# A normalised layer with a spectral filter, a code correction and an FFN: another order of DVE's and ACT's work in the first two chunks, and one pair of sums moved from POOL to DVE

## The chip, the cores and the metric

One core of a Trainium2 chip runs the kernel. The metric is the device time of one execution in microseconds.

## The reference

The input x is 2 x 4096 tokens of 256 numbers. With `xn = layernorm(x)` over the 256 numbers, the result is `x + attn(xn) + ffn(xn)`:

- `ffn`: `gelu(xn @ w1 + b1) @ w2 + b2`, 256 to 1024 to 256.
- `attn`: a number D (a "fractal dimension") is computed from the first 1024 numbers of `xn`: for five prefix lengths, the count of values over the prefix's mean, and a slope of logarithms. D gives a filter of 256 frequencies; `x1` is the inverse FFT of the filtered FFT of every row, a circulant matrix product. 24 latents `x1 @ W_el + b_el` are cut to bits at zero, corrected by a code with 12 checks, and `attn = x1 + corrected @ W_le + b_le`.

## The kernel before

**Tiling.** The 8192 tokens are worked in 16 chunks of 512 (CTOK). A chunk is held transposed: 128 partitions x 2 halves of the row (KB) x 512 tokens. The 1024 hidden units are 8 blocks (MB), numbered m. To get fp32 accuracy, both factors of a product are split in a high part (a cast to fp32r, by ACT) and a low part (the subtraction, by DVE), and PE multiplies hi*hi, lo*hi and hi*lo.

**PE's order.** `up(c, par, m)` (L857, matmuls on L882) makes block m of the hidden layer of chunk c in p_h, and `down(c, m)` (L887, L900 and L905) adds it to p_f, two blocks later. In between stand `latents` (L919, L926: the 24 latents into p_l), `filtered` (L930: the circulant product into p_s), `checks` (L941: the code's products) and `le_products` (L952, L956: the corrected bits by W_le, added to p_s). Each engine runs its own list in program order; semaphores join them. Chunk 0 runs in an opening of its own (L1046 to L1075) in which the filter is being made, chunk 1 in `first_branch_chunk`, which also does the latents, the filter and the corrections of chunk 0; then a loop `chunk` does two chunks a turn, and `last_chunk` ends.

**What ACT, DVE and POOL do.** ACT: Gelu (L433), the high part of the hidden block (L441, `hidden_hi`), high part of the chunk's columns xn (L411, `columns_hi`), of uv (L418, `turned_hi`), the weights' high parts (L481, L486). DVE: the low parts: `hidden_lo` (L611), `columns_lo` (L601), `turned_lo` (L606), `w1_part_lo` (L732); the statistics of the next chunk (L569) and `aggregate` (L574); `centre` (L591) and `scale` (L596), which normalise the columns; `add_ffn` (L635), which adds p_f to the output and frees p_f for the next chunk; `take_bits` (L616), which cuts p_l to bits and frees p_l; `take_checks` (L628), `correct` (L623), and the additions of p_s. POOL: `inverse_root` (L346 to L351: 1/sqrt(var + eps) by a power) and `turn` (L363: uv, the sum and the difference of the two halves of the columns). SP issues the DMAs in its own order; `spread_rows` (L268) writes mean and 1/std to DRAM and reads them back broadcast to all partitions (L286).

**The opening on DVE and ACT.** The two lists are written out by hand: DVE's L750 to L844, ACT's L489 to L542. DVE mixes chunk 0's low parts with the filter's scalar steps (L782 to L811), the weights' low parts, and the preparation of chunk 1. The latents' rows are `le_t` (W_le's sums and differences, L822), split in three bf16 parts: le3 first part on ACT (L516), the rest `le_r1` on DVE (L828), `le_mid` and its copy on ACT (L540, L542), the last part on DVE (L842). `c_hi` and `c_lo` (L532, L834) are the circulant matrix, `cw` (L536 on ACT, L837 on DVE) the latents' weights by it; the latter's `c_ready` lets PE start `latents(0)`. `columns_lo(1, 1)` lets PE start `up(1, ...)`: its wait is on `t_lo` (L861). `latents(1)` waits for `bits_done` of chunk 0 (L922), `down(1, 0)` for `ffn_added` of chunk 0 (L892), `le_products(0)` for `cor_done` (L954). `xc0` are the columns of chunk 0, copied by ACT (L510) into rows_sb[0].

Of the kernel before, what the change touches and what calls it, by code (L numbers as in the profile page):

```python
# [8 lines left out]
ALU = mybir.AluOpType  # L9
# [4 lines left out]
TOKENS, E, HID, LAT, SYN = 2 * 4096, 256, 1024, 24, 12  # L14
# [54 lines left out]
def build(nc, x, xt, small, latent, w1, w2, ident, consts, basis, codes, out):  # L69
    ctx = ExitStack()  # L70
    with ctx:
# [17 lines left out]
        xc0 = rows_sb[0]  # L89
# [237 lines left out]
        def _(pool):  # L327
# [23 lines left out]
                nc.gpsimd.tensor_tensor(row_nums[par][:, 1, tiles], var_eps[:, tiles], minus_half[:, tiles],  # L351
                                        ALU.pow).then_inc(rstd_done, 1)

            def turn(c, first=False):

                if first:
                    pool.wait_ge(xc0_made, 1)
                else:
                    pool.wait_ge(scaled, c)
                    pool.wait_ge(u_lo, c)  # L360
                columns = xc0 if first else xn
                for k, op in enumerate((ALU.add, ALU.subtract)):
                    nc.gpsimd.tensor_tensor(uv[:, k, :], columns[:, 0, :], columns[:, 1, :], op).then_inc(turned, 1)  # L363


            for g in range(2):
# [21 lines left out]
            then(nc.gpsimd.tensor_tensor(series[:], series[:], weighted[:], ALU.mult))  # L388
            nc.gpsimd.tensor_tensor(filt_w[:], series[:, 0:KB], series[:, KB:2 * KB], ALU.mult).then_inc(filt_made, 1)

            turn(0, first=True)
            inverse_root(2 + HEAD, 0)
            turn(1)
            with pool.Fori(0, (CHUNKS - 4) // 2) as i:
# [8 lines left out]
        def _(act):  # L403
# [4 lines left out]
            def columns_hi(c, par):  # L408

                act.wait_ge(scaled, c)  # L410
                nc.scalar.copy(xT_hi[par][:, :, :], xn[:, :, :]).then_inc(t_hi, 1)  # L411
# [99 lines left out]
            last.then_inc(xc0_made, 1)  # L511
            gelu(0, 4, first=True)
            hidden_hi(0, 4, first=True)
            act.wait_ge(le_turned, 1)
            act.wait_ge(le_set, 1)
            nc.scalar.mul(le3[0:LAT, :, :], le_t[:], 0.5).then_inc(le_first, 1)  # L516
            gelu(0, 5, first=True)
            hidden_hi(0, 5, first=True)
            act.wait_ge(code_in, 16)
# [10 lines left out]
            made = p_l[:, 0:E].rearrange("p (a e) -> p a e", a=2)  # L530
            nc.scalar.copy(c_f[:, :, :], made).then_inc(c_copied, 1)
            nc.scalar.copy(c_hi[:, :, :], made).then_inc(c_hi_ready, 1)  # L532
            act.wait_ge(cw_made, 1)
            act.wait_ge(cw_set, 1)
            latent_made = p_g[:, SEG:SEG + KB * LAT].rearrange("p (k l) -> p k l", k=KB)
            nc.scalar.copy(cw[:, :, 0:LAT], latent_made).then_inc(cw_hi_ready, 1)  # L536
            columns_hi(1, 1)
            turned_hi(0, first=True)
            act.wait_ge(le_rest, 1)
            nc.scalar.copy(le_mid[:], le_r1[:]).then_inc(le_second, 1)  # L540
# [11 lines left out]
        def _(dve):  # L552
# [61 lines left out]
            def take_bits(c, par):  # L614
                dve.wait_ge(rest_done, c + 1)
                nc.vector.scalar_tensor_tensor(out=word[SEG * par:SEG * par + LAT, :], in0=p_l[0:LAT, :],  # L616
                                               scalar=latent_sb[:, 0:1], in1=rest[:],
                                               op0=ALU.add, op1=ALU.is_gt).then_inc(bits_done, 1)
# [12 lines left out]
            def add_ffn(c):  # L631
                dve.wait_ge(down_done, MB * (c + 1))
                for k in range(KB):
                    xc = columns(c)[:, k, :]
                    nc.vector.scalar_tensor_tensor(out=xc, in0=p_f[:, k, :], scalar=bias[:, k:k + 1], in1=xc,  # L635
                                                   op0=ALU.add, op1=ALU.add).then_inc(ffn_added, 1)
# [39 lines left out]
            def first_branch_chunk(c, par):  # L676
                b = c - 1
                statistics(c + 1, 1 - par)
                add_ffn(b)
                dve.wait_ge(stats_made, c + HEAD + 2)  # L680
                hidden_lo(c, 0)
                aggregate(1 - par)
                take_bits(b, 1 - par)
                hidden_lo(c, 1)
                hidden_lo(c, 2)
                turned_lo(c)
                take_checks(b)
                take_bits(c, par)
                hidden_lo(c, 3)
                centre(c + 1, 1 - par)  # L690
                scale(c + 1, 1 - par)
                hidden_lo(c, 4)
                correct(b)
                take_checks(c)
                columns_lo(c + 1, 1 - par)
                hidden_lo(c, 5)
                add_sums(b)
                hidden_lo(c, 6)
                add_differences(b)
                hidden_lo(c, 7)  # L700
# [64 lines left out]
            for g in range(2):  # L765
# [22 lines left out]
            then(nc.vector.tensor_tensor(fr_b[:], values, fr_s[:, 1, :].unsqueeze(2).broadcast_to(table), ALU.is_gt))  # L788
            then(nc.vector.tensor_tensor(fr_a[:], fr_b[:], masks, ALU.mult))
            nc.vector.tensor_reduce(fr_s[:, 2, :], fr_a[:], AX.X, ALU.add).then_inc(part_counts, 1)  # L790
            statistics(1, 1)
            hidden_lo(0, 1)
            w1_part_lo(2)
            dve.wait_ge(stats_made, 3)
            aggregate(1)
            hidden_lo(0, 2)
# [27 lines left out]
                                    ALU.subtract).then_inc(le_turned, 1)  # L824
            hidden_lo(0, 5)
            hidden_lo(0, 6)
            dve.wait_ge(le_first, 1)
            nc.vector.scalar_tensor_tensor(out=le_r1[:], in0=le_t[:], scalar=0.5, in1=le3[0:LAT, :, :],  # L828
                                           op0=ALU.mult, op1=ALU.subtract).then_inc(le_rest, 1)
            centre(1, 1)  # L830
            scale(1, 1)
            hidden_lo(0, 7)
            dve.wait_ge(c_hi_ready, 1)
            nc.vector.tensor_tensor(c_lo[:, :, :], c_f[:, :, :], c_hi[:, :, :].bitcast(F32), ALU.subtract)  # L834
            dve.wait_ge(cw_hi_ready, 1)
            latent_made = p_g[:, SEG:SEG + KB * LAT].rearrange("p (k l) -> p k l", k=KB)
            nc.vector.tensor_tensor(cw[:, :, SEG:SEG + LAT], latent_made, cw[:, :, 0:LAT].bitcast(F32),  # L837
                                    ALU.subtract).then_inc(c_ready, 1)
            columns_lo(1, 1)
            turned_lo(0)  # L840
            dve.wait_ge(le_second, 1)
            nc.vector.tensor_tensor(le3[2 * SEG:2 * SEG + LAT, :, :], le_r1[:], le_mid[:],  # L842
# [342 lines left out]
```

## Time and profile before

| | us |
|---|---|
| median of 3 runs | 418.75 (418.73 to 419.31) |
| the profiled execution, its own time | 418.89 |
| its span in the trace | 417.1 |
| PE busy | 409.1 (98%) |
| DVE busy | 307.3 (74%) |
| ACT busy | 218.7 (52%) |
| POOL busy | 73.7 (18%) |
| share of PE in the chain that ended last | 93% |

The span is the stretch from the first to the last instruction of the trace; the profiled execution took 1.8 us more than its span. The clock that PE was granted was 0.999 of its full speed over the span. In a timeline a row is one or several instructions of one kind in a row, with start and duration; brackets say how long the engine stood idle before it and what released it. Durations of successive instructions overlap a little, so that the pace is read from start to start.

### The profile page before, as it was taken

What the parts mean: (1) busy time and instruction counts of PE and PEld (TensorE: products, weight loads), DVE (VectorE), ACT (ScalarE), POOL (GpSimd) and SP (SyncE); (2) the same over time, 40 slices, a digit from 0 to 9 for tenths busy, and PEclk for the clock granted to TensorE, in tenths of its full rate; (3) what the DMA queues carried; (4) which work ended last, traced back from release to release, by engine and by line L of the source; (5) the groups of instructions that cost most, each with busy time, mean ns of one, the idle gap of its engine ahead of it and who ended that gap; (6) DMA issues with size and microseconds to landing.
All of it is one profiled execution on the core that took longest, in us unless ns stands there. A gap on an engine that the chain in (4) does not pass through costs nothing.

```text
span 417.1 us, 5569 instructions
## 1 busy us (share of the span) xinstructions
PE 409.1 (98%) x1789; PEld 325.8 (78%) x1789; DVE 307.3 (74%) x503; ACT 218.7 (52%) x325; POOL 73.7 (18%) x102
## 2 busy tenths in 40 slices
PE   8998999999999999999999999999999999999996
PEld 4786787887888788787887878788787878878774
DVE  7888696968669686776867778686786868676654
ACT  3957446555365554536555464554536655464641
POOL 2161321212012121111212012121111212012000
PEclk9999999999999999999999999999999999999999
DMA  7562223133331123332122332223333111111011
GB/s 221 200 210 95 101 61 92 52 101 103 101 101 56 51 95 101 101 101 72 53 76 101 101 101 90 26 86 101 101 101 98 53 51 51 51 51 50 2 50 50
DMA packets 16495, 36.04 MB, mean 86 GB/s; under 512 B 5452, under 2 KB 8164, under 8 KB 16484
## 3 DMA queue, kind: packets, MB, share of 16 engines
q1 hardware_dynamic: 16340, 35.78, 27.2%
q10 hardware_dynamic: 144, 0.13, 0.1%
q8 instruction: 5, 0.08, 0.1%
q14 instruction: 6, 0.05, 0.1%
HBM read 27.45 MB, written 8.45 MB: 86 GB/s over the span
## 4 chain that ended last, share of the span: by engine, by line
PE 93%; DVE 4%; DMA 1%; issue 1%; ACT 0%; POOL 0%; SPq 0%; DVEq 0%
PE p_h L882 41%; PE p_f L900 27%; PE p_f L905 13%; PE p_s L937 5%; PE p_l L926 3%; PE p_s L956 2%; PE p_g L950 1%; DMA x_sb<-x 1%; DVE stats L569 1%; DVE xt_sb L644 0%; DVE xt_sb L650 0%; DVE xT_lo L601 0%; DVE w_lo L732 0%; DVE h_lo L611 0%; DVE xt_sb L726 0%
## 5 line engine op out<-in xcount | busy, mean ns | idle before, releaser
L433 ACT ACTIVATE h<-p_h,small_sb 128x512 f32<-128x512 f32 x128 | 88.1, 688 | 155.1 <-PE p_h L882 155.0
L611 DVE TENSOR_TENSOR h_lo<-h,h_hi 128x512 fp32r<-128x512 f32 x128 | 90.1, 704 | 71.4 <-ACT h_hi L441 71.2
L900 PE MATMUL p_f<-h_hi,w_hi 128*128 128x512 f32 x254 | 99.7, 392 | 0.0
L900 PE MATMUL p_f<-h_hi,w_lo 128*128 128x512 f32 x254 | 99.0, 390 | 0.0
L882 PE MATMUL p_h<-xT_hi,w_hi 128*128 128x512 f32 (+1 forms) x258 | 86.1, 415 | 1.5 <-DVE xT_lo L601 1.0
L441 ACT CAST h_hi<-h 128x512 fp32r<-128x512 f32 x128 | 79.4, 620 | 5.8
L882 PE MATMUL p_h<-xT_lo,w_hi 128*128 128x512 f32 (+1 forms) x258 | 79.6, 390 | 0.1
L882 PE MATMUL p_h<-xT_hi,w_lo 128*128 128x512 f32 (+1 forms) x258 | 79.5, 389 | 0.0
L905 PE MATMUL p_f<-h_lo,w_hi 128*128 128x512 f32 x254 | 78.2, 389 | 0.0
L363 POOL TENSOR_TENSOR uv<-xn 128x512 f32<-128x512 f32 x30 | 43.6, 1475 | 127.7 <-DVE xn L596 127.7
L882 PEld LDWEIGHTS p_h<-xT_hi,w_hi 128*128 128x128 f32 x258 | 48.3, 189 | 11.9 <-DVE xT_lo L601 1.5
L882 PEld LDWEIGHTS p_h<-xT_lo,w_hi 128*128 128x128 f32 x258 | 48.3, 188 | 10.8 <-DVE xT_lo L767 0.3
L882 PEld LDWEIGHTS p_h<-xT_hi,w_lo 128*128 128x128 f32 x258 | 48.3, 188 | 10.7
L900 PEld LDWEIGHTS p_f<-h_hi,w_hi 128*128 128x128 f32 x254 | 47.7, 188 | 10.3
L905 PEld LDWEIGHTS p_f<-h_lo,w_hi 128*128 128x128 f32 x254 | 47.7, 188 | 10.1
L900 PEld LDWEIGHTS p_f<-h_hi,w_lo 128*128 128x128 f32 x254 | 47.7, 188 | 10.0
L346 POOL TENSOR_TENSOR var_eps<-mv,eps 128x4 f32<-128x4 f32 (+1 forms) x17 | 3.9, 227 | 173.3 <-DVE mv L574 173.3
L601 DVE TENSOR_TENSOR xT_lo<-xn,xT_hi 128x1024 fp32r<-128x1024 f32 x15 | 32.7, 2179 | 0.8 <-ACT xT_hi L411 0.7
L635 DVE SCALAR_TENSOR_TENSOR xt_sb<-p_f,bias,xt_sb 128x512 f32 (+1 forms) x30 | 21.1, 746 | 12.5 <-PE p_f L905 12.5
L606 DVE TENSOR_TENSOR uv_lo<-uv,uv_hi 128x1024 fp32r<-128x1024 f32 x16 | 19.6, 1226 | 9.2 <-ACT uv_hi L418 9.2
L411 ACT CAST xT_hi<-xn 128x1024 fp32r<-128x1024 f32 x15 | 15.8, 1054 | 13.5 <-DVE xn L596 13.5
L591 DVE TENSOR_TENSOR xn<-xt_sb,rows_sb 128x1024 f32<-128x1024 f32 x15 | 18.3, 1223 | 5.9 <-DMA rows_sb<-rows_dram 5.5
(117 smaller groups left out, 331.4 us busy)
## 6 DMA issues: line engine op xcount, KB each, us to landing
xt_sb<-xt SPq DMA_DIRECT2D x16, 512.0 KB, 5.2
x_sb<-x SPq DMA_DIRECT2D x15, 512.0 KB, 4.5
rows_sb<-rows_dram SPq DMA_DIRECT2D x15, 512.0 KB, 4.1
out<-xt_sb SPq DMA_DIRECT2D x15, 512.0 KB, 2.9
xt_sb<-w SPq DMA_DIRECT2D x3, 512.0 KB, 7.3
xt_sb<-w SPq DMA_DIRECT2D x2, 256.0 KB, 4.1
basis_sb<-basis SPq DMA_DIRECT2D x1, 384.0 KB, 8.8
x_sb<-x SPq DMA_DIRECT2D x2, 128.0 KB, 2.1
```

The costliest lines, as they stand in the source:

```text
L363: nc.gpsimd.tensor_tensor(uv[:, k, :], columns[:, 0, :], columns[:, 1, :], op).then_inc(turned, 1)
L433: nc.scalar.activation(h[m % 2][:], p_h[:, m % 2, :], ACT.Gelu, bias=small_sb[:, S_B1 + m:S_B1 + m + 1]).then_inc(gelu_done, 1)
L441: nc.scalar.copy(h_hi[m % HR][:], h[m % 2][:]).then_inc(h_hi_done, 1)
L591: nc.vector.tensor_tensor(xn[:, :, :], columns(c), to_halves(rows_sb[par][:, 0, :]), ALU.subtract).then_inc(centred, 1)
L601: nc.vector.tensor_tensor(xT_lo[par][:, :, :], xn[:, :, :], xT_hi[par][:, :, :].bitcast(F32), ALU.subtract).then_inc(t_lo, 1)
L606: nc.vector.tensor_tensor(uv_lo[:, :, :], uv[:, :, :], uv_hi[:, :, :].bitcast(F32), ALU.subtract).then_inc(u_lo, 1)
L611: nc.vector.tensor_tensor(h_lo[m % HR][:], h[m % 2][:], h_hi[m % HR][:].bitcast(F32), ALU.subtract).then_inc(h_lo_done, 1)
L635: nc.vector.scalar_tensor_tensor(out=xc, in0=p_f[:, k, :], scalar=bias[:, k:k + 1], in1=xc, op0=ALU.add, op1=ALU.add).then_inc(ffn_added, 1)
L882: last = mm(p_h[:, m % 2, tok], w[:, k, m * P:(m + 1) * P], xp[par][:, k, tok], start=(n == 0), stop=(n == 3 * KB - 1))
L900: mm(p_f[:, a, :], w[:, m, a * HF:(a + 1) * HF], h_hi[r][:], start=(m == 0 and w is w2_hi), stop=False, skip_group_check=True)
L905: last = mm(p_f[:, a, :], w2_hi[:, m, a * HF:(a + 1) * HF], h_lo[r][:], start=False, stop=(m == MB - 1), skip_group_check=True)
L937: last = mm(p_s[:, k, :], w[:, k, :], xp[:, k, :], start=(n == 0), stop=False, skip_group_check=True)
```

## The change

On POOL, `turn(0)` is gone; DVE makes the two sums of chunk 0 itself. On ACT, the first part of the latents' rows (le3, `le_first`) is made after `columns_hi(1, 1)`, which itself stands ahead of the wait for `cw_made`. On DVE, in the opening: `w1_part_lo(2)` and `hidden_lo(0, 1)` stand ahead of `statistics(1, 1)`; `le_r1` is made after `cw`, `columns_lo(1, 1)` before it, with the two sums between. In `first_branch_chunk`, `add_ffn(0)` stands after `take_bits(0)`.

```diff
--- before.py
+++ after.py
@@ -351,16 +351,12 @@
                 nc.gpsimd.tensor_tensor(row_nums[par][:, 1, tiles], var_eps[:, tiles], minus_half[:, tiles],
                                         ALU.pow).then_inc(rstd_done, 1)
 
-            def turn(c, first=False):
-
-                if first:
-                    pool.wait_ge(xc0_made, 1)
-                else:
-                    pool.wait_ge(scaled, c)
-                    pool.wait_ge(u_lo, c)
-                columns = xc0 if first else xn
+            def turn(c):
+
+                pool.wait_ge(scaled, c)
+                pool.wait_ge(u_lo, c)
                 for k, op in enumerate((ALU.add, ALU.subtract)):
-                    nc.gpsimd.tensor_tensor(uv[:, k, :], columns[:, 0, :], columns[:, 1, :], op).then_inc(turned, 1)
+                    nc.gpsimd.tensor_tensor(uv[:, k, :], xn[:, 0, :], xn[:, 1, :], op).then_inc(turned, 1)
 
 
             for g in range(2):
@@ -388,7 +384,6 @@
             then(nc.gpsimd.tensor_tensor(series[:], series[:], weighted[:], ALU.mult))
             nc.gpsimd.tensor_tensor(filt_w[:], series[:, 0:KB], series[:, KB:2 * KB], ALU.mult).then_inc(filt_made, 1)
 
-            turn(0, first=True)
             inverse_root(2 + HEAD, 0)
             turn(1)
             with pool.Fori(0, (CHUNKS - 4) // 2) as i:
@@ -511,9 +506,6 @@
             last.then_inc(xc0_made, 1)
             gelu(0, 4, first=True)
             hidden_hi(0, 4, first=True)
-            act.wait_ge(le_turned, 1)
-            act.wait_ge(le_set, 1)
-            nc.scalar.mul(le3[0:LAT, :, :], le_t[:], 0.5).then_inc(le_first, 1)
             gelu(0, 5, first=True)
             hidden_hi(0, 5, first=True)
             act.wait_ge(code_in, 16)
@@ -530,11 +522,14 @@
             made = p_l[:, 0:E].rearrange("p (a e) -> p a e", a=2)
             nc.scalar.copy(c_f[:, :, :], made).then_inc(c_copied, 1)
             nc.scalar.copy(c_hi[:, :, :], made).then_inc(c_hi_ready, 1)
+            columns_hi(1, 1)
+            act.wait_ge(le_turned, 1)
+            act.wait_ge(le_set, 1)
+            nc.scalar.mul(le3[0:LAT, :, :], le_t[:], 0.5).then_inc(le_first, 1)
             act.wait_ge(cw_made, 1)
             act.wait_ge(cw_set, 1)
             latent_made = p_g[:, SEG:SEG + KB * LAT].rearrange("p (k l) -> p k l", k=KB)
             nc.scalar.copy(cw[:, :, 0:LAT], latent_made).then_inc(cw_hi_ready, 1)
-            columns_hi(1, 1)
             turned_hi(0, first=True)
             act.wait_ge(le_rest, 1)
             nc.scalar.copy(le_mid[:], le_r1[:]).then_inc(le_second, 1)
@@ -676,11 +671,11 @@
             def first_branch_chunk(c, par):
                 b = c - 1
                 statistics(c + 1, 1 - par)
-                add_ffn(b)
                 dve.wait_ge(stats_made, c + HEAD + 2)
                 hidden_lo(c, 0)
                 aggregate(1 - par)
                 take_bits(b, 1 - par)
+                add_ffn(b)
                 hidden_lo(c, 1)
                 hidden_lo(c, 2)
                 turned_lo(c)
@@ -788,9 +783,9 @@
             then(nc.vector.tensor_tensor(fr_b[:], values, fr_s[:, 1, :].unsqueeze(2).broadcast_to(table), ALU.is_gt))
             then(nc.vector.tensor_tensor(fr_a[:], fr_b[:], masks, ALU.mult))
             nc.vector.tensor_reduce(fr_s[:, 2, :], fr_a[:], AX.X, ALU.add).then_inc(part_counts, 1)
+            w1_part_lo(2)
+            hidden_lo(0, 1)
             statistics(1, 1)
-            hidden_lo(0, 1)
-            w1_part_lo(2)
             dve.wait_ge(stats_made, 3)
             aggregate(1)
             hidden_lo(0, 2)
@@ -824,19 +819,23 @@
                                     ALU.subtract).then_inc(le_turned, 1)
             hidden_lo(0, 5)
             hidden_lo(0, 6)
-            dve.wait_ge(le_first, 1)
-            nc.vector.scalar_tensor_tensor(out=le_r1[:], in0=le_t[:], scalar=0.5, in1=le3[0:LAT, :, :],
-                                           op0=ALU.mult, op1=ALU.subtract).then_inc(le_rest, 1)
             centre(1, 1)
             scale(1, 1)
             hidden_lo(0, 7)
             dve.wait_ge(c_hi_ready, 1)
             nc.vector.tensor_tensor(c_lo[:, :, :], c_f[:, :, :], c_hi[:, :, :].bitcast(F32), ALU.subtract)
+            columns_lo(1, 1)
+
+            dve.wait_ge(xc0_made, 1)
+            for k, op in enumerate((ALU.add, ALU.subtract)):
+                nc.vector.tensor_tensor(uv[:, k, :], xc0[:, 0, :], xc0[:, 1, :], op).then_inc(turned, 1)
             dve.wait_ge(cw_hi_ready, 1)
             latent_made = p_g[:, SEG:SEG + KB * LAT].rearrange("p (k l) -> p k l", k=KB)
             nc.vector.tensor_tensor(cw[:, :, SEG:SEG + LAT], latent_made, cw[:, :, 0:LAT].bitcast(F32),
                                     ALU.subtract).then_inc(c_ready, 1)
-            columns_lo(1, 1)
+            dve.wait_ge(le_first, 1)
+            nc.vector.scalar_tensor_tensor(out=le_r1[:], in0=le_t[:], scalar=0.5, in1=le3[0:LAT, :, :],
+                                           op0=ALU.mult, op1=ALU.subtract).then_inc(le_rest, 1)
             turned_lo(0)
             dve.wait_ge(le_second, 1)
             nc.vector.tensor_tensor(le3[2 * SEG:2 * SEG + LAT, :, :], le_r1[:], le_mid[:],
```

## Rows read from the trace of the kernel before

**Rows 1.** Table by stage for PE: stretch, PE busy, matmuls, granted clock, DMA share, GB/s.

```profile
16.00:42.00 26.00, 24.00 (x110) 1.00 0.38 124
42.00:392.00 350.00, 350.00 (x1533) 1.00 0.25 78
```

**Rows 2.** Timeline of PE around its three gaps: start, duration, line, tiles, idle before.

```profile
15.86 0.28 PE L1042 MATMUL p_g<-fr_s,ones 128*128 128x5 f32 x2
16.59 0.73 PE L882 MATMUL p_h<-xT_hi,w_hi 128*128 128x512 f32 x2 [0.46 <-DVE w_lo L732]
...
19.43 0.28 PE L1042 MATMUL p_g<-fr_d,ones 128*128 128x1 f32 x2
19.57 0.71 PE L882 MATMUL p_h<-xT_hi,w_hi 128*128 128x512 f32 x2
...
33.33 0.62 PE L905 MATMUL p_f<-h_lo,w_hi 128*128 128x512 f32 x2
34.98 0.73 PE L882 MATMUL p_h<-xT_hi,w_hi 128*128 128x512 f32 x2 [1.02 <-DVE xT_lo L601]
35.54 0.62 PE L882 MATMUL p_h<-xT_hi,w_lo 128*128 128x512 f32 x2
...
39.69 0.61 PE L882 MATMUL p_h<-xT_lo,w_hi 128*128 128x512 f32 x2
40.82 0.73 PE L926 MATMUL p_l<-xT_hi,cw 128*128 128x512 f32 x2 [0.52 <-DVE word L616]
41.40 0.62 PE L926 MATMUL p_l<-xT_lo,cw 128*128 128x512 f32 x2
41.86 0.40 PE L937 MATMUL p_s<-uv_hi,c_hi 128*128 128x512 f32 x1
```

**Rows 3.** Timeline of ACT, the same columns.

```profile
13.36 0.61 ACT L481 CAST w_hi<-xt_sb 128x512 fp32r<-128x512 f32 x1
...
23.18 0.42 ACT L516 ACTIVATE le<-le_t 24x256 bf16<-24x256 f32 x1 [2.53 <-DVE le_t L823]
...
29.20 0.38 ACT L532 CAST c_hi<-p_l 128x256 fp32r<-128x256 f32 x1
...
44.85 1.05 ACT L418 CAST uv_hi<-uv 128x1024 fp32r<-128x1024 f32 x1 [2.20 <-POOL uv L363]
```

**Rows 4.** DVE's L611 from 24 to 34 us: ns min/median/max, first and last start.

```profile
L611 DVE TENSOR_TENSOR h_lo<-h,h_hi x3: 687/1766/1776, 24.9 to 31.0; 128x512 fp32r<-128x512 f32 x3
```

**Rows 5.** POOL's L363, ns min/median/max and starts, and its timeline in chunk 1.

```profile
L363 POOL TENSOR_TENSOR uv<-rows_sb x2: 1291/1519/1747, 24.8 to 26.0; 128x512 f32<-128x512 f32 x2
...
42.23 2.58 POOL L363 TENSOR_TENSOR uv<-xn 128x512 f32<-128x512 f32 x2
```

**Rows 6.** Timeline of DVE from 28 to 53 us.

```profile
28.58 1.21 DVE L591 TENSOR_TENSOR xn<-xt_sb,rows_sb 128x1024 f32<-128x1024 f32 x1
...
33.70 1.23 DVE L601 TENSOR_TENSOR xT_lo<-xn,xT_hi 128x1024 fp32r<-128x1024 f32 x1 [0.74 <-ACT xT_hi L411]
...
36.54 1.40 DVE L569 BATCH_NORM_STATS2 stats<-x_sb 128x6 f32<-128x256 f32 x4
37.86 1.39 DVE L635 SCALAR_TENSOR_TENSOR xt_sb<-p_f,bias,xt_sb 128x512 f32<-128x512 f32 x2
...
40.06 0.71 DVE L616 SCALAR_TENSOR_TENSOR word<-p_l,latent_sb,rest 24x512 bf16<-24x512 f32 x1
...
45.93 1.23 DVE L606 TENSOR_TENSOR uv_lo<-uv,uv_hi 128x1024 fp32r<-128x1024 f32 x1 [3.52 <-ACT uv_hi L418]
...
52.29 0.68 DVE L623 TENSOR_SCALAR cor<-p_g 96x512 bf16<-96x512 uint32 x1
```

**Rows 7.** SP's broadcast of the rows' numbers (L286): issue ns, first start, us to landing.

```profile
L286 SPq DMA_DIRECT2D rows_sb<-rows_dram x15: 319/320/333, 21.1 to 368.7; - x15
...
DMA to landing us min/median/max: 3.6/4.1/4.9
```

**Rows 8.** PE's timeline where chunk 0's corrections are multiplied.

```profile
53.36 0.60 PE L956 MATMUL p_s<-cor,le 96*128 96x512 bf16 x2
```

## The prediction

> **What bounds the kernel now.** I read the table by stage first. From 42 to 392 us PE is busy in 350.00 of 350 us, at a granted clock of 1.00; from 16 to 42 us it is busy in 24.00 of 26 us [rows 1]. So the loop is a solid block of matmuls, and whatever PE gains before 42 us it keeps to the end, as long as nothing else falls behind. The 2.00 us missing from 16 to 42 us are three gaps, which PE's timeline shows in brackets: 0.46 us ahead of `up(0, 4)`, released by the low part of w1; 1.02 us ahead of `up(1, 0)`, released by `columns_lo(1)`; 0.52 us ahead of `latents(1)`, released by `take_bits(0)` [rows 2]. All three wait for DVE. The change touches exactly the DVE work ahead of each.
>
> **What a gap costs.** Idle time understates it, because a matmul behind a wait also hides nothing of its weights' load. I therefore go from start to start. First gap: after the two 5-column matmuls the next start comes 0.73 us later (15.86 to 16.59); the same pair with no wait behind it takes 0.14 us (19.43 to 19.57). Loss 0.59. Second: 33.33 to 34.98 is 1.65, and 34.98 to 35.54 is 0.56, where two pairs without a wait are 0.46 apart (41.40 to 41.86); 1.65 + 0.56 - 0.92 = 1.29. Third: 39.69 to 40.82 is 1.13, then 0.58 to 41.40; 1.71 - 0.92 = 0.79 [rows 2]. The sum is 2.67 us by starts and 2.00 by idle brackets; I take 2.67, since starts are what shifts the block behind, and keep 2.00 as the lower bound of what three closed gaps bring.
>
> **Part 1, w1's low part ahead of hidden_lo(0, 1) and statistics(1).** ACT has the high part at 13.36 + 0.61 = 13.97 [rows 3]. In the order before, four statistics (1.3 us start to start, as 36.54 to 37.86 [rows 6]) and one `hidden_lo` (0.6 to 0.69) stand ahead of it; without them the low part is ready some 1.9 us earlier, at about 14.7, where PE wants it at 16.59 - 0.59 = 16.0. The gap closes, gain 0.59. `hidden_lo(0, 1)` also comes earlier; the statistics end at about 16.5 where the low part ended before, so everything behind them on DVE stays where it was. PE then reaches its later steps 0.59 earlier; by the timeline of DVE I expect none of them to be late.
>
> **Part 2, POOL's sums of chunk 0 go.** POOL made them from 24.8 us on, in 1291 and 1747 ns [rows 5]. Beside them two `hidden_lo` took 1766 and 1776 ns where the third of the same shape took 687 [rows 4]. I read this as the two engines hindering each other: 2 x 1.08 = 2.16 us of DVE's time. With POOL silent this is saved, and it lies on the path to the second gap. The page SBUF — State Buffer of the Trainium skill (section Who interferes with whom) says that a DVE instruction with two SBUF inputs and a GpSimd instruction that reads SBUF exclude one another, whichever is first holding the other up; by that rule the rows are two instructions taking turns, and the trace agrees in its size (a delay of 1.08 beside a POOL operation of 1.29).
>
> **Part 3, ACT.** ACT stood idle for 2.53 us before le3's first part, for `le_t` [rows 3]. Moved back, this wait no longer holds up the Gelu of block 5, and with it blocks 6 and 7 and the scaling of the basis. PE does not wait for them either way, so in itself it is worth nothing; it lets DVE have `hidden_lo(0, 5)` and `(0, 6)` done between 25.4 and, if ACT gained nothing on block 6, 27.1. The 0.42 of le3 now sits behind `columns_hi(1)`, in ACT's wait for `cw_made`, where ACT has nothing else.
>
> **Part 4, chunk 1's columns.** `centre(1)` needs the broadcast rows: issued at 21.1, landing 3.6 to 4.9 later [rows 7], so at 26.0 at the latest. It began at 28.58 [rows 6] and can now begin at 25.4 to 27.1. With `scale` it takes 2.45 (each as the 1.21), so xn is there at 27.9 to 29.5. ACT is free for `columns_hi(1)` when c_hi is made, which PE sets: 29.20 + 0.38 - 0.59 = 28.99 [rows 3]. The cast takes 1.05, as uv's does [rows 3], so 30.0; `columns_lo` 1.23 [rows 6], done at 31.2, or at 31.8 at the latest by the bounds above. PE wants it at 33.79 - 0.59 = 33.2. The second gap closes with 1.4 to 2.0 us to spare; gain 1.29.
>
> **Part 5, the sums on DVE.** No row shows them there. The nearest is `hidden_lo`, the same 128x512 in fp32 with two SBUF inputs: 0.687, which I take (0.6 start to start); the upper bound is a pair held up by another engine, 1.776 [rows 4], the lower nothing. They stand from 31.1 to 32.4. Behind them wait: `cw`'s low part, on which `latents(0)` hangs (ready at 32.6 or so, wanted 1.4 after `up(1, 0)`, at 34.6: covered); ACT's `turned_hi(0)`, 32.4 to 33.5; `turned_lo(0)`, then le's last part, `statistics(2)`. From `columns_lo` to the statistics it was 36.54 - 33.70 = 2.84 [rows 6]; less one subtraction of 1.14 start to start, 1.7 remain, so the statistics start at 33.5 + 1.7 = 35.2 instead of 36.54. le_r1 (0.33) falls into DVE's wait for uv_hi. SP's broadcast for chunk 2 waits for `turned` too, but before that for chunk 2's 1/std, which is later.
>
> **Part 6, add_ffn behind take_bits.** Between the statistics and the bits stood 40.06 - 36.54 = 3.52 us, of which add_ffn about 1.31 (its two of 0.7) [rows 6]. Without it the bits start at 35.2 + 2.2 = 37.4 and are there at 38.1. PE, 1.88 us earlier than before, wants them at 40.15 - 1.88 = 38.27. That is the tightest point of the sum: the margin is 0.1 to 0.2, and the weights' load wants to start 0.2 before. I count 0.1 lost and 0.69 gained. add_ffn then runs until 39.5; `down(1, 0)` wants it after `latents(1)` and `filtered(0)` (0.93 + 1.4), at 40.6. Covered by 1.1.
>
> **What is late next.** POOL's `turn(1)` hangs on `aggregate`, which moves with the bits. From the bits' start to `turned_lo(1)` it was 45.93 - 40.06 = 5.87, with 2.20 of ACT's wait for POOL in it; from there DVE ran without a pause to `correct(0)`, done 7.04 later at 52.97 [rows 3, 6]. PE used it at 53.36 [rows 8], 0.39 later. Now: 37.4 + 5.87 + 7.04 = 50.3, wanted at 53.36 - 2.67 = 50.7. The margin stays 0.4, if POOL takes no longer. It took 2.58 beside an idle DVE [rows 5], and will now meet `hidden_lo(1, 1)` and `(1, 2)`; its first pair took 1291 + 1747 beside such work, so up to 0.4 more: just covered. By the rule of the page named above, two `hidden_lo` would each wait for a POOL operation, which delays them but no product of PE; add_ffn, with one large SBUF input, would not be held.
>
> **The sum.** 0.59 + 1.29 + 0.69 = 2.57. The profiled execution took 418.89, so 416.3; the median of the runs is 0.14 under it, so 416.2 in the median. A difference of 0.2% (0.84 us) is about what a measurement of this kernel can tell from none.
>
> **Rivals.**
> A, the forecast: 416.2, with 415.9 if the third gap vanishes whole and the pairs run a little closer, 416.75 if only the bracketed idle time (2.00) comes back. Chance 0.70.
> B, bits still late: `take_bits(0)` takes the third gap's place because the sums, ACT's cast and `turned_lo` in front of the statistics come out 0.5 to 1 us longer than my sum of nine steps. Against it, each has its row. Time 418.75 - 1.88 to 418.75 - 2.1: 416.7 to 417.1. Chance 0.14.
> C, a new wait at `le_products(0)` or `down(1, 0)`: the margin of 0.4 is spent because POOL and DVE hold each other up around 39 to 43 us. If add_ffn is held for two POOL operations (2 x 1.29 less the margin of 1.1), 1.5 us come back as a wait: 417.7. If only turn(1) is slower by 0.8, 0.4 comes back: 416.6. Chance 0.08.
> D, DVE's 1.77 was not POOL's doing but that of the DMA then running: then the two `hidden_lo` stay slow and the sums take 1.77 each, 2.3 more than counted. `centre` at 26.6 to 27.1, bits at 40.5, third gap 2.3 instead of 0.79: the total gain is 0.3 us, 418.4. Against it: `centre` at 28.58 took its ordinary 1.21 [rows 6] while loads were under way. Chance 0.05. That the change moves no gap at all is in this case.
> E, slower: the sums on DVE are each held up by an operation as long as POOL's longest, 0.69 + 1.75 = 2.44. Place: between `columns_lo(1)` and `turned_lo(0)`. Every step from there to the bits moves 2 x (2.44 - 0.6) = 3.7; less the margin of 0.1 the third gap becomes 3.6 and the gain is 2.67 - 3.7 = -1.0: 419.8. It decides from 1.9 to 2.0 us a sum upward. Against it: POOL has no instruction between the filter's last and chunk 2's inverse root, so there is no one to hold them up. Chance 0.03.
>
> **The numbers.** The likeliest case gives 416.2. The range takes in A and B, and the milder half of C: 415.8 to 417.3. Faster by over 0.2% (under 417.9) are A, B and most of C: 0.91. Within 0.2%: D and the worst of C, 0.06. Slower: E, 0.03.
>
> **What the profile after would show.** Right: PE without a bracket at `up(0, 4)` and `up(1, 0)`, and one of at most 0.2 at `latents(1)`; busy 26.00 of 26 us at 16 to 42, or nearly; the two `hidden_lo` of blocks 5 and 6 at 0.69; DVE's sums at 0.69 each by 32.5 us; bits at 37.4; no wait of PE at L956 and L900; PE's block from 62 us on unchanged and 2.6 us earlier. Wrong, if a gap of over 0.3 us stands at `latents(1)` (B), at L956 or at `down(1, 0)` (C), if `hidden_lo` stays at 1.77 (D), or if the loop has gaps that it hasn't now.

## The result, and the profile after

| | before | after |
|---|---|---|
| median of 22 runs each, us | 418.88 (418.68 to 419.42) | 417.61 (416.46 to 420.66) |
| profiled execution: its time, its span | 418.89, 417.1 | 417.44, 415.6 |
| PE busy | 409.1 | 407.7 |
| DVE, ACT, POOL busy | 307.3, 218.7, 73.7 | 309.0, 218.9, 73.0 |

The ratio is 0.9973, 95% interval 0.9966 to 0.998: the change is faster, by 1.27 us, where the forecast was 2.6. The measured median lies 0.3 us above the range. The runs of the changed kernel also scatter more.

Table by stage for PE of the changed kernel, the columns of [rows 1]:

```profile
16.00:42.00 26.00, 25.13 (x114) 1.00 0.38 125
42.00:392.00 350.00, 350.00 (x1533) 1.00 0.25 78
```

The loop is still solid. From 16 to 42 us 0.87 us are missing where 2.00 were, and all of it is one new gap. PE's timeline of the changed kernel, with the starts that answer to [rows 2] (every line number is one lower):

```profile
15.77 0.28 PE L1041 MATMUL p_g<-fr_s,ones 128*128 128x5 f32 x2
15.90 0.71 PE L881 MATMUL p_h<-xT_hi,w_hi 128*128 128x512 f32 x2
...
26.75 0.61 PE L904 MATMUL p_f<-h_lo,w_hi 128*128 128x512 f32 x2
28.23 1.13 PE L1024 MATMUL p_l<-basis_w,basis_sb 128*128 128x256 f32 x4 [0.87 <-ACT basis_w L518]
29.01 0.59 PE L899 MATMUL p_f<-h_hi,w_hi 128*128 128x512 f32 x1
...
33.80 0.62 PE L904 MATMUL p_f<-h_lo,w_hi 128*128 128x512 f32 x2
34.25 0.62 PE L881 MATMUL p_h<-xT_hi,w_hi 128*128 128x512 f32 x2
...
38.88 0.61 PE L881 MATMUL p_h<-xT_lo,w_hi 128*128 128x512 f32 x2
39.38 0.73 PE L925 MATMUL p_l<-xT_hi,cw 128*128 128x512 f32 x2
39.95 0.63 PE L925 MATMUL p_l<-xT_lo,cw 128*128 128x512 f32 x2
...
51.90 0.61 PE L955 MATMUL p_s<-cor,le 96*128 96x512 bf16 x2
```

The product of the basis by the filter's weights, which makes the circulant matrix (L1024, called the circulant product from here on), stood without a gap in the kernel before:

```profile
27.41 0.62 PE L905 MATMUL p_f<-h_lo,w_hi 128*128 128x512 f32 x2
27.87 1.03 PE L1025 MATMUL p_l<-basis_w,basis_sb 128*128 128x256 f32 x4
28.55 0.59 PE L900 MATMUL p_f<-h_hi,w_hi 128*128 128x512 f32 x1
```

Laid beside the starts of before, PE's lead grows and shrinks in steps. It is 0.09 us at 15.77, which is luck of the opening. The first gap is closed: +0.60. Ahead of the circulant product the lead is 0.66 us (26.75 against 27.41); behind it PE is 0.46 us late (29.01 against 28.55): -1.12. The second gap is closed: +1.29. The third is closed but for 0.15: +0.63. With 0.03 lost in between, that leaves 1.46 us at `le_products(0)` (53.36 against 51.90). So the three terms of the sum were 0.60, 1.29 and 0.63 where 0.59, 1.29 and 0.69 were forecast, and a fourth, -1.12, was missing.

Where it comes from stands in the timelines of POOL, ACT and DVE of the changed kernel:

```profile
22.88 1.08 POOL L376 TENSOR_TENSOR quads<-quads,con 128x16 f32<-128x16 f32 x1
...
24.75 0.69 POOL L382 TENSOR_TENSOR series<-halves,powers 128x4 f32<-128x4 f32 x1
...
26.08 1.10 POOL L385 TENSOR_TENSOR filt_w<-series 128x2 f32<-128x2 f32 x1
```

```profile
27.27 0.91 ACT L518 ACTIVATE basis_w<-basis_sb,filt_w 128x256 f32<-128x256 f32 x2 [2.61 <-POOL filt_w L385]
```

```profile
23.21 0.67 DVE L606 TENSOR_TENSOR h_lo<-h,h_hi 128x512 fp32r<-128x512 f32 x1
24.69 0.69 DVE L606 TENSOR_TENSOR h_lo<-h,h_hi 128x512 fp32r<-128x512 f32 x1 [0.81 <-ACT h_hi L436]
25.90 1.23 DVE L586 TENSOR_TENSOR xn<-xt_sb,rows_sb 128x1024 f32<-128x1024 f32 x1 [0.51 <-DMA rows_sb<-rows_dram]
```

POOL makes the filter in twelve small steps. Three of them, of 16, 4 and 2 columns, took 1.08, 0.69 and 1.10 us; each is open while a wide DVE subtraction with two inputs in SBUF runs, and ends just behind it (23.88 + 0.08, 25.38 + 0.06, 27.13 + 0.05). Their neighbours take 0.20. POOL's starts say the same as its durations: the step behind the first of the three starts 1.16 us after it (24.04), in e1 below 0.35 (23.18 to 23.53). In the kernel before the same three steps took 0.27, 0.20 and 0.19, and from 23.15 to 24.86 DVE stood idle behind ACT, which had waited for `le_t` [rows 3]; POOL, then DVE:

```profile
20.59 1.11 POOL L376 TENSOR_TENSOR powers<-angle 128x4 f32<-128x4 f32 x1 [2.01 <-DVE angle L811]
21.78 0.52 POOL L377 TENSOR_TENSOR powers<-powers 128x4 f32<-128x4 f32 x1
...
22.74 0.27 POOL L380 TENSOR_TENSOR quads<-quads,con 128x16 f32<-128x16 f32 x1
...
24.64 0.19 POOL L389 TENSOR_TENSOR filt_w<-series 128x2 f32<-128x2 f32 x1
```

```profile
20.43 1.22 DVE L738 TENSOR_TENSOR w_lo<-xt_sb,w_hi 128x1024 fp32r<-128x1024 f32 x1
21.56 0.69 DVE L611 TENSOR_TENSOR h_lo<-h,h_hi 128x512 fp32r<-128x512 f32 x1
...
24.86 3.47 DVE L611 TENSOR_TENSOR h_lo<-h,h_hi 128x512 fp32r<-128x512 f32 x2 [1.70 <-ACT h_hi L441]
```

DVE's subtraction began at 24.86, when the filter was made (24.83). Now ACT begins the Gelu of block 5 2.9 us earlier (20.58 against 23.51), DVE follows, the filter is late (27.18), ACT scales the basis late and PE waits.

These rows also show that the filter's path was held up already in the kernel before. Its first two steps, of 4 columns each, took 1.11 and 0.52 us and ended 0.05 us behind DVE's w_lo (21.65) and `hidden_lo` (22.25), both wide and with two SBUF inputs. They have these lengths, and end 0.05 to 0.06 us behind DVE's, in the traces of all fourteen kernels here, e1 too. Measured against the usual 0.20 that is 1.2 us, an estimate from these rows; no run took them apart from DVE's work.

### The profile page after: what moved, and what is told of

Read it like the earlier page. It is cut to its first block, busy times and chain, and to the rows that moved or that the text cites. A ratio compares the mean times of both kernels' runs of the same rounds, so it can differ in the third digit from the quotient of the medians.

```text
span 415.6 us, 5569 instructions
## 1 busy us (share of the span) xinstructions
PE 407.7 (98%) x1789; PEld 325.6 (78%) x1789; DVE 309.0 (74%) x505; ACT 218.9 (53%) x325; POOL 73.0 (18%) x100
## 3 DMA queue, kind: packets, MB, share of 16 engines
HBM read 27.45 MB, written 8.45 MB: 86 GB/s over the span
## 4 chain that ended last, share of the span: by engine, by line
PE 96%; DVE 1%; DMA 1%; POOL 0%; issue 0%; ACT 0%; DVEq 0%; SPq 0%; ACTq 0%; POOLq 0%
PE p_h L881 43%; PE p_f L899 28%; PE p_f L904 14%; PE p_s L936 5%; PE p_l L925 4%; PE p_s L955 2%; PE p_g L949 1%; DMA x_sb<-x 1%; POOL row_nums L351 0%; DVE xt_sb L639 0%; DVE xt_sb L645 0%; DVE xt_sb L721 0%; PE p_l L1024 0%; DVE rows_sb L740 0%; PE p_s L1054 0%
## 5 line engine op out<-in xcount | busy, mean ns | idle before, releaser
L359 POOL TENSOR_TENSOR uv<-xn 128x512 f32<-128x512 f32 x30 | 44.5, 1502 | 128.1 <-DVE xn L591 128.1
```

Of the source, the lines that this page charges most:

```text
L359: nc.gpsimd.tensor_tensor(uv[:, k, :], xn[:, 0, :], xn[:, 1, :], op).then_inc(turned, 1)
```

## The experiments

In the table, "opening taken out" is the time on PE from the first 5-column product (12.86 us in the trace before) to `le_products(0)` (53.36), which leaves out what differs before the first and includes all three old gaps. Each is from one trace. The ratios are against runs of the kernel before in the same rounds, whose medians were 418.78 to 418.97.

| kernel | median, us | ratio, 95% interval | opening taken out, us |
|---|---|---|---|
| before | 418.88 | | 40.50 |
| the change | 417.61 | 0.9973, 0.9966 to 0.998 | 39.13 |
| e1, filter first | 416.44 | 0.9940, 0.9926 to 0.9954 | 38.09 |
| e2, filter before centre | 417.04 | 0.9953, 0.9940 to 0.9967 | 38.23 |
| e3, latents' rows back | 417.40 | 0.9965, 0.9951 to 0.9978 | 38.99 |
| e7, e1 with POOL's sums | 416.47 | 0.9946, 0.9932 to 0.9959 | 38.12 |
| e4, columns only | 417.72 | 0.9976, 0.9966 to 0.9985 | 39.38 |
| e5, w1 only | 418.57 | 0.9995, 0.9986 to 1.0004 | 40.16 |
| e6, bits first only | 418.21 | 0.9986, 0.9977 to 0.9995 | 39.94 |
| e10, those three together | 417.38 | 0.9957, 0.9943 to 0.9970 | 38.60 |
| e11, sums only | 418.92 | 0.9997, 0.9988 to 1.0007 | 40.52 |
| e12, latents' rows only | 418.84 | 0.9996, 0.9984 to 1.0007 | 40.48 |
| e8, two SBUF inputs | 417.81, one run | | 39.52 |
| e9, one PSUM input | 416.71, one run | | 38.01 |

### Is it DVE's work that delays the filter?

**e1** adds one wait to the changed kernel:

```diff
+            dve.wait_ge(filt_made, 1)
             hidden_lo(0, 5)
             hidden_lo(0, 6)
```

Expected: 

> The changed kernel, with one wait more on DVE: hidden_lo(0, 5) of the first chunk waits until POOL has made the filter. Theory (POOL's filter steps are held up by DVE's two-input subtractions, 2.35 us in the changed kernel, and PE waits for the scaled basis for 1.13 us): filter at 25.0 instead of 27.2 us, all of POOL's small steps at 0.2 us, no wait of PE ahead of the circulant product, time 1.1 us under the changed kernel, about 416.4 to 416.6 us, and a narrower spread of the runs. Rival (the delay of the filter is POOL's own, or comes from DMA): filter still at 27, time 417.6 or more, since DVE is now idle as well.

POOL's same three steps in e1, and DVE behind them:

```profile
23.18 0.28 POOL L376 TENSOR_TENSOR quads<-quads,con 128x16 f32<-128x16 f32 x1
...
24.25 0.20 POOL L382 TENSOR_TENSOR series<-halves,powers 128x4 f32<-128x4 f32 x1
...
25.09 0.20 POOL L385 TENSOR_TENSOR filt_w<-series 128x2 f32<-128x2 f32 x1
```

```profile
25.32 1.29 DVE L606 TENSOR_TENSOR h_lo<-h,h_hi 128x512 fp32r<-128x512 f32 x2 [1.73 <-POOL filt_w L385]
```

```profile
16.00:42.00 26.00, 26.00 (x120) 1.00 0.38 126
```

DVE now stands idle for 1.73 us ahead of these two, and the kernel is 1.2 us faster than the change: 416.44, 0.2 above what was forecast for the change. PE is busy in 26.00 of 26 us, and no time goes at the circulant product (1.14 us from the pair ahead of it to the matmul behind it, as before). The five runs lie within 0.4 us. Not all of POOL's small steps are short, as was expected: the first two keep 1.11 and 0.52.

**e2** puts the same wait two lines lower, behind `hidden_lo(0, 6)`.

Expected: 

> The changed kernel, with DVE waiting for the filter only after hidden_lo(0, 6), before centre(1). Theory: the last POOL step keeps its 0.2 us instead of 1.10, the two earlier ones stay long (1.08 and 0.69), filter at about 26.3, PE waits 0.1 to 0.3 ahead of the circulant product: about 416.7 us, between e1 and the changed kernel. Rival as in e1: no gain, 417.6.

```profile
22.95 1.08 POOL L376 TENSOR_TENSOR quads<-quads,con 128x16 f32<-128x16 f32 x1
...
24.82 0.72 POOL L382 TENSOR_TENSOR series<-halves,powers 128x4 f32<-128x4 f32 x1
...
26.18 0.20 POOL L385 TENSOR_TENSOR filt_w<-series 128x2 f32<-128x2 f32 x1
```

Two steps stay long, the third, which had met `centre(1)`, is short, and PE loses 0.23 us at the circulant product, too little for a bracket. The median, 417.04, is between e1 and the change, so that half of the loss is gone by the medians. By the one trace, which is of a run of 416.61, 0.90 of 1.04 us is gone (38.23 against 39.13 and 38.09). What the slower runs of e2 lose isn't shown.

**e8 and e9** ask which DVE work does it. Both are e1 with two additions into an unused tile in DVE's idle time; they differ in one operand (each kernel has one of the two lines marked e8 and e9):

```diff
+            dve.wait_ge(xc0_made, 1)
+            for k in range(KB):
+                nc.vector.tensor_tensor(scrap[:, k, :], xc0[:, 1 - k, :], xc0[:, k, :], ALU.add)   # e8
+                nc.vector.tensor_tensor(scrap[:, k, :], p_s[:, k, :], xc0[:, k, :], ALU.add)       # e9
             dve.wait_ge(filt_made, 1)
```

Expected of e8: 

> e1 with two more DVE additions of 128x512 ahead of its wait for the filter, at about 23.2 to 24.5 us, both inputs in SBUF, results unused. Theory of exclusion: one or two of POOL's small steps grow by 0.5 to 0.7 us each, the filter comes at 25.6 to 26.4, one of the additions may take longer. Rival: no effect on POOL.

Expected of e9: 

> As e8, but one input of each addition is in PSUM. Theory of exclusion by the second SBUF input: POOL's steps keep 0.2 us, the filter at 25.0 as in e1. Rival (any DVE work hinders POOL): as in e8.

The additions and the POOL step beside them, e8 and then e9:

```profile
23.06 1.68 POOL L377 TENSOR_TENSOR quads<-quads,con 128x16 f32<-128x16 f32 x1
...
23.39 1.27 DVE L823 TENSOR_TENSOR scrap<-rows_sb 128x512 f32<-128x512 f32 x2
```

```profile
23.29 0.27 POOL L377 TENSOR_TENSOR quads<-quads,con 128x16 f32<-128x16 f32 x1
...
23.63 1.27 DVE L823 TENSOR_TENSOR scrap<-p_s,rows_sb 128x512 f32<-128x512 f32 x2
```

With both inputs in SBUF a POOL step of 0.27 us waits through both additions, 1.68 us, and the filter comes at 26.58, a little later than expected. With one input in PSUM the POOL steps that follow at the same time (23.64 to 25.39) all keep 0.20, the filter comes at 25.39, and the additions take the same 1.27. It is not DVE being busy; it is the second SBUF input. DVE's additions lose nothing here. SBUF — State Buffer of the Trainium skill states in Who interferes with whom that a DVE instruction with two SBUF inputs contends with a GpSimd instruction that reads SBUF, and that one with at most one SBUF input, outside the two-port modes (which `tensor_tensor` hasn't), does not; e8 and e9 agree with both halves. Downstream e8 loses 0.54 us at the circulant product, and the bits are late (a wait of 0.87 at `latents(1)`), which is the same delay handed on through DVE's own wait.

### Which parts of the change were worth something?

**e3** is the changed kernel with the three lines of le3's first part back ahead of `gelu(0, 5)`.

Expected: 

> The changed kernel, with the latents' first rows on ACT back ahead of Gelu block 5 of the first chunk (one part of the change undone). Theory: ACT then hands DVE blocks 5 and 6 at 24.9 and 26.4, after POOL's filter steps, which keep 0.2 us each; the basis is in time; DVE's own chain ends later, so that the gap at latents(1) is 0.4 to 0.6: about 416.7 to 416.9 us. Rival (ACT's earlier Gelu is what closes the gap at up(1, 0)): a gap comes back there, 417.6 or more.

POOL's steps are short again (filter at 24.97), since `hidden_lo(0, 5)` starts at 25.00. In return DVE's chain ends later:

```profile
39.10 0.73 PE L925 MATMUL p_l<-xT_hi,cw 128*128 128x512 f32 x2 [0.45 <-DVE word L611]
```

By its bracket the gap is of the size expected; from start to start it costs 0.72 us, where e7 loses 0.04 there and the change 0.15. Another 0.22 goes at the circulant product, for which ACT, with the latents' rows in front, has the basis ready only as PE wants it (27.32 against 27.26), and 0.19 before it, mostly at `up(0, 7)` (24.36 and 24.95). The median, 417.40, is therefore above the 416.7 to 416.9 expected. By its trace e3 is 0.14 us better than the change (38.99 against 39.13), by its median 0.2, which the intervals don't separate. So the move of the latents' rows costs PE 0.7 us up to the circulant product (1.12 against 0.22 + 0.19) and gives back 0.6 at `latents(1)` (0.15 against 0.72): on balance about nothing, but as the difference of a cost that the forecast left out and a gain on DVE's chain.

**e7** is e1 with the change's other large part undone, POOL makes chunk 0's sums behind the filter.

Expected: 

> e1, but POOL makes chunk 0's two sums again, after the filter, as in the kernel before. Theory A (the sums on POOL cost DVE 2.2 us on the path to the columns of chunk 1): hidden_lo of blocks 5 and 6 take 1.77 each again, columns_lo ends near 33 where PE wants it at 33.2, but DVE saves the 1.2 us of sums behind it: 0 to 0.5 us slower than e1, 416.4 to 417.0. Theory B (the move of the sums is what brought the gain): 417.7 or more.

```profile
25.05 3.45 DVE L611 TENSOR_TENSOR h_lo<-h,h_hi 128x512 fp32r<-128x512 f32 x2 [1.71 <-POOL filt_w L389]
28.42 1.21 DVE L591 TENSOR_TENSOR xn<-xt_sb,rows_sb 128x1024 f32<-128x1024 f32 x1
...
32.01 1.23 DVE L601 TENSOR_TENSOR xT_lo<-xn,xT_hi 128x1024 fp32r<-128x1024 f32 x1 [0.17 <-ACT xT_hi L411]
```

The subtractions are slow again and the columns are ready at 33.24, just when PE wants them (33.2), which costs 0.25 us from start to start at `up(1, 0)`; the 1.2 us that DVE saves behind them make up for it: the bits start as long after the opening as in e1 (37.63 - 12.78 against 37.86 - 13.06), and 0.04 us is lost at `latents(1)` where e1 loses 0.22. The median is e1's within the noise. So the move of the sums is worth nothing that these runs can tell once the filter is protected.

**e11** is the kernel before with the sums alone moved to DVE, behind `c_lo`; **e4** the kernel before with chunk 1's columns alone moved:

```diff
             nc.scalar.copy(c_hi[:, :, :], made).then_inc(c_hi_ready, 1)
+            columns_hi(1, 1)
             act.wait_ge(cw_made, 1)
...
-            columns_hi(1, 1)
...
             nc.vector.tensor_tensor(c_lo[:, :, :], c_f[:, :, :], c_hi[:, :, :].bitcast(F32), ALU.subtract)
+            columns_lo(1, 1)
...
-            columns_lo(1, 1)
```

Expected of e11: 

> The kernel before, with only the two sums of chunk 0 moved from POOL to DVE, behind c_lo. Theory: hidden_lo of blocks 5 and 6 fall from 1.77 to 0.69 us and centre starts 1.5 to 2 us earlier, but ACT's columns_hi(1) still stands behind the wait for the latents' weights (32.6): the gap at up(1, 0) stays at 1.0, time as before, 418.7 to 418.9. Rival (the prediction's step: the 2.16 us saved lie on the path to that gap): the gap closes, 417.5.

Expected of e4: 

> The kernel before, with only chunk 1's columns moved: on ACT columns_hi(1) ahead of the wait for the latents' weights, on DVE columns_lo(1) behind c_lo. POOL keeps the sums. Theory (in the kernel before ACT's order held the columns back, not POOL's sums on DVE): columns_hi at 31.1 instead of 32.6, the gap ahead of up(1, 0) closes (1.29), the gap at latents(1) stays at 0.7 to 0.8: 417.5 us. Rival, as the prediction put it (the 2.2 us of slow subtractions lie on that path): little gain, 418.5 or more.

e11, timelines of DVE, ACT and PE:

```profile
26.39 0.69 DVE L606 TENSOR_TENSOR h_lo<-h,h_hi 128x512 fp32r<-128x512 f32 x1 [0.85 <-ACT h_hi L436]
27.00 0.41 DVE L823 SCALAR_TENSOR_TENSOR le_r<-le_t,le 24x256 f32<-24x256 f32 x1
27.33 1.21 DVE L586 TENSOR_TENSOR xn<-xt_sb,rows_sb 128x1024 f32<-128x1024 f32 x1
```

```profile
32.65 1.05 ACT L406 CAST xT_hi<-xn 128x1024 fp32r<-128x1024 f32 x1
```

```profile
35.01 0.73 PE L881 MATMUL p_h<-xT_hi,w_hi 128*128 128x512 f32 x2 [1.02 <-DVE xT_lo L596]
```

e4, ACT and PE:

```profile
30.97 1.05 ACT L411 CAST xT_hi<-xn 128x1024 fp32r<-128x1024 f32 x1 [1.46 <-DVE xn L596]
```

```profile
33.72 0.62 PE L882 MATMUL p_h<-xT_hi,w_hi 128*128 128x512 f32 x2
```

In e11 DVE's subtractions are fast, its columns xn are ready 1.25 us earlier, and the gap stays at 1.02: ACT stood behind its wait for the latents' weights. In e4 ACT's cast starts at 30.97 instead of 32.61 with POOL's sums still in place, and the gap is gone (PE's pair starts at 33.72 with no bracket); the median is 417.72, 1.1 us better than before in the same rounds, and a little above the 417.5 expected, since the gap at `latents(1)` grows to 0.91 from start to start. The rival of e4, which was the prediction's own view of that path, is refuted. e4 moved the columns on both engines; the move on ACT alone was not tried.

**e12** is the kernel before with the latents' rows alone moved back, on both engines.

Expected: 

> The kernel before, with only the latents' first rows moved back on ACT and DVE. Theory: ACT's Gelu of block 5 comes 2.5 us earlier, DVE's subtractions of blocks 5 and 6 then fall on POOL's filter steps, two or three of which grow by 0.5 to 0.8; the filter comes at 26.2 to 27.0 instead of 24.8, PE waits 0 to 0.4 us for the basis; this part by itself gains nothing: 418.7 to 419.2, the wait absorbed in part by the gap at up(1, 0). Rival (an earlier Gelu only helps): filter at 24.8, 418.75 or less.

Two of POOL's steps grow (1.08 and 0.67), POOL's sums then take 4.56 us and hold up DVE's `scale` and `hidden_lo(0, 7)` (2.19 and 1.78). PE loses nothing of it: the filter ends 13.24 us after the first 5-column product (11.97 in the kernel before, 14.41 in the change), and ACT has the basis ready at 28.93 where PE uses it at 29.70. With two collisions instead of three, and the first gap still open, that is in time. The trace is of the outlier of 420.67 (see the last section), so its times stand 1.8 us late throughout, which the table leaves out. The median is that of before, 418.84: alone this part gains nothing.

**e5** has w1's low part and `hidden_lo(0, 1)` alone ahead of the statistics; **e6** add_ffn(0) alone behind the bits.

Expected of e5: 

> The kernel before, with only w1's third low part and hidden_lo(0, 1) ahead of the statistics. Theory: the gap ahead of up(0, 4) closes and everything behind moves with PE: 0.6 us faster, 418.2 to 418.3. Rival (the gap comes back at up(1, 0), whose wait then grows): 418.8.

Expected of e6: 

> The kernel before, with only add_ffn(0) behind take_bits(0). Theory: bits 1.3 us earlier, the gap at latents(1) closes whole (0.79), le_products(0) in time since aggregate and POOL's turn move too: 418.0 to 418.1. Rival (add_ffn then holds up down(1, 0)): 418.8.

e6 gained 0.6 us in the medians of its rounds (418.21 against 418.78), a little less than expected. The gap at `latents(1)` is closed whole (its pairs start at 39.52, 39.98 and 40.45), but 0.2 us comes back at `le_products(0)`, as in e10 below: the corrections end at 52.49 and PE starts at 52.63. In e5 the first gap is closed, but the median gains 0.2 us only, and the interval includes no gain at all. Its trace, of a run of 418.87, shows two things. The opening was later: the first part of w1 landed so that ACT's cast began at 7.36 us instead of 6.31, and PE's first 5-column product came at 13.17 instead of 12.86. In the other traces that cast began between 5.95 and 7.40. And `up(1, 0)` came at 34.97, only 0.01 earlier than before: of the lead of 0.28 that was left behind the first gap, 0.25 went at the circulant product (27.15 to 28.54 against 27.41 to 28.55), as in e3: PE, now earlier, finds ACT's basis hardly ready. The second gap stays as it was, at 1.02. Whether this opening is typical for e5 or chance, one trace doesn't show.

**e10** is the kernel before with the edits of e4, e5 and e6 together: no sums moved, no latents' rows moved.

Expected: 

> The kernel before with three of the five parts: w1's low part forward, chunk 1's columns forward, add_ffn(0) behind the bits. POOL keeps the sums of chunk 0, ACT keeps the latents' rows ahead of Gelu block 5, so that hidden_lo of blocks 5 and 6 stay behind POOL's filter steps and take 1.77 each beside POOL's sums. Theory: those three close all three gaps and nothing delays the filter: 416.4 to 416.7 us, faster than the full change (417.6), with the gap at latents(1) closed since no sums stand ahead of turned_lo(0). Rival (the sums must leave POOL for the gap at up(1, 0) to close): a gap of 0.5 to 1.0 stays there, 417.2 or more.

All three gaps are closed (25.99 of 26 us), with two parts of the change left out; opening taken out, it is 0.5 us better than the whole change. Its median is 417.38, above the 416.4 to 416.7 that was expected, and its interval overlaps that of the change. The trace shows what is missing against e7 (38.12): 0.2 us goes at the circulant product without a bracket, as in e3 and e5, and 0.2 at `le_products(0)`, whose corrections come too late; the opening of this one trace is 0.43 later besides:

```profile
39.46 4.04 POOL L363 TENSOR_TENSOR uv<-xn 128x512 f32<-128x512 f32 x2
...
50.98 0.68 DVE L623 TENSOR_SCALAR cor<-p_g 96x512 bf16<-96x512 uint32 x1
```

POOL's `turn(1)` took 4.04 us here, 3.42 in the changed kernel and 2.58 before [rows 5], because it now meets `hidden_lo(1, 1)` and `(1, 2)`. The corrections end at 51.66 where PE was ready at 51.6, and PE starts at 51.81.

## Why the prediction was wrong

**The rows and the frame held.** Three gaps, nothing lost from 42 us on, losses counted from start to start and not by idle time: the three terms came out at 0.60, 1.29 and 0.63. Had idle brackets been summed, they would have given 2.00; in e1 and e7 2.4 came back, the 2.57 of the forecast less what stayed behind at `latents(1)` or `up(1, 0)`.

**The step that failed is part 3.** "PE does not wait for them either way, so in itself it is worth nothing" looked only at who waits for ACT. It did not ask what DVE would do with blocks 5 and 6 handed over 2.9 and 1.7 us earlier. The term that it put at nothing measured -1.12 us at the circulant product, and e1, whose one wait keeps DVE's subtractions behind the filter, gives 1.17 back in the median. The prediction had read the rule of mutual exclusion from [rows 4, 5] and used it twice, where POOL's sums slow DVE, and where `turn(1)` would meet DVE. It did not look for a third place, the one in which POOL works on PE's path: the filter's steps, the last of which in the trace before stand in a DVE idle time of 1.7 us, while the first two are held up already. None of the rivals was this one, and none of the signs of being wrong names a gap at the circulant product. E said that POOL had no instruction to hold DVE up between filter and inverse root, which is true; the hold-up came just ahead of that, and in the other direction. "PE does not wait for them either way" also fails the other way round: once the first gap is closed and the latents' rows stay in front, PE loses 0.20 to 0.25 us to ACT's scaling of the basis (e3, e5, e10).

**Part 2 was right in its size and wrong in its place.** The two subtractions fell from 1.77 to 0.67 and 0.69 as said. But "it lies on the path to the second gap" is refuted by e11 (gap unchanged) and e4 (gap closed without it). What held up the second gap was the order on ACT, `columns_hi(1)` behind the wait for `cw_made`. With that order mended the slow subtractions do come close to the path (ACT waits 1.46 us for xn in e4), and in e7 and e10 they cost 0.25 and 0.29 us there, not 1.29. The prediction did count on that move in part 4, so the sum came out right with a wrong credit.

**Parts 1, 4, 5 and 6.** The low part of w1 was ready at 14.64, where 14.7 was forecast. `centre(1)` started at 25.90, inside 25.4 to 27.1, by the DMA's landing; `columns_lo` ended at 32.24 instead of 31.2 because c_hi was late with the circulant product; the sums took 1.28 for two, as the nearest row said. The bits started at 38.61 instead of 37.4 and PE came 1.1 late too, so that the third gap came out 0.06 worse than forecast. add_ffn held up nothing.

**What is late next.** Right in the changed kernel: `correct(0)` ended 0.27 before PE used it, where 0.4 was forecast. POOL's `turn(1)` grew by 0.84, twice what was allowed for; it was covered because the power step before it, no longer beside a `hidden_lo`, took 1.02 instead of 1.75. e6 and e10, in which turn(1) took 4.03 and 4.04 us, show that margin used up, at 0.2 us each: a mild form of rival C.

**The range.** Rival B's upper end of 417.1 doesn't follow from its own sum, in which 418.75 - 1.88 is 416.9. The result would lie above the range either way.

**The scatter.** Runs of the change spread from 416.46 to 418.8 with one at 420.66, those of before and of e1 over 0.7 and 0.4 us. That the spread comes from which POOL step meets which DVE instruction fits the narrow spread of e1 and the wider one of e2 (0.8), but there is one trace only of the changed kernel, so it is not shown.

## To carry to other kernels

When work is moved earlier, look at what runs beside its new place on the engine it shares SBUF reads with, and above all whether small steps there stand on the critical path: three POOL steps of 0.2 to 0.3 us cost 2.2 us together. A small step that takes several times as long as its neighbours and ends with the other engine's instruction is the sign; the trace of before had two. An idle time of an engine may be what protects another; one added wait, e1, gained nearly as much as the whole change (1.17 and 1.27 us). And before crediting a gain to a faster instruction, find the last wait ahead of the gap, on every engine between.

## What was not expected of the hardware

- A POOL `tensor_tensor` of 128x16 that starts before DVE's wide two-input one by 0.3 us can still wait for it, and for the next one behind it (1.68 us in e8 for both). By the recorded starts the small step was first, and would have ended 0.06 us before the wide one began, and still lost. In e4 a 128x4 step that started 0.47 us ahead of a `hidden_lo` took 1.21 us, where the same step as far ahead of it took 0.20 in the kernel before. How the two are ordered inside was not settled.
- DVE's instruction that meets such a small POOL step loses next to nothing (0.67 to 0.69), while beside POOL's 128x512 operations it takes 1.77. In these rows what either loses goes with the other's length.
- In e12's profiled execution, an outlier (420.67), the granted clock fell at the start, here beside the same stretch of before:

```profile
8.00:12.00 4.00, 3.55 (x18) 0.62 0.98 341
```

```profile
8.00:12.00 4.00, 3.93 (x25) 1.00 0.97 335
```

PE had stood idle for 1.13 us up to 7.21 and for 0.61 up to 8.45, waiting for the first normalised rows; the granted clock was 0.98 from 8 to 9 us and 0.50 from 9 to 12, which is the lower of its two levels (1.2 and 2.4 GHz), and 0.91 from 12 to 14. The first 5-column product came 1.8 us late (14.68 against 12.86), which is the whole of the outlier's excess over the median. The other outliers, 420.51 to 420.66 in the change, in e12 and twice in before, have a mean clock of 0.995 or 0.996 over the span, like this one, and nearly all other runs 0.997 or more; that they are the same thing is likely by that and not shown. Waits of 1.45 and 0.29 us at the same places in the changed kernel's trace, and of 1.21 and 0.61 in e9's, were followed by a full clock, so the length of the waits alone does not decide it.
